# Turning tiles between the slices of the weights product, 32 turns of the identity first, and single loads for the third pair's mixed words

## The chip, the cores and the metric

One Trainium2 chip, one of its NeuronCores. The metric is the device time of one execution of the whole kernel, in microseconds. The core's engines are TensorE (PE), VectorE (DVE), ScalarE (ACT) and GpSimd (POOL); SyncE (SP) issues all DMAs of this kernel, one after the other, and waits on semaphores in between, so that a DMA whose condition isn't met holds all that stand behind it.

## What is computed

Tokens are 2048 rows of 1024 numbers, float32 throughout. The reference, cut to what matters:

```python
xn = _layernorm(x)                                  # over 1024
# gated part
s = silu(xn @ w_gate.T)                             # 2752 columns
# per row, the half of s with the smallest magnitudes is set to 0
idx = top_k(-abs(s), 1376); s[rows, idx] = 0
attn = (s * (xn @ w_up.T)) @ w_down.T
# shared and routed part
logits = xn @ gate_w                                # 8 experts
h = relu(xn @ up_w) ** 2                            # 2048 columns
shared = h @ down_w
routed = ((xn @ fc1_w) @ expert_w * sum(top_k(logits, 2))) @ fc2_w
y = x + attn + (layernorm(shared + routed) * gamma + beta)
```

## The kernel before

Tokens go in four blocks of 512. A block's products run over *granules*: 128 rows of a weight matrix by 512 columns, multiplied by all 512 tokens (four tiles of 128). Full float32 accuracy is had with three passes at the fast float32r rate: each operand is split into a high part (rounded by ScalarE) and a low part (the rest, by GpSimd or VectorE), and `product` (L943 to L947) multiplies high by high, high by low and low by high into one PSUM bank. `plan.granules` is the list of a block's granules in the order of TensorE; the number `m` of a granule in it is what all tables of the program are indexed by. I call it the granule's **place**. Every engine walks over the same places in its own loop and does at each what the tables name there; only semaphores tie the engines together, so VectorE, say, may be some places ahead of TensorE.

**Start.** Before block 0, `expert_w @ fc2_w` (512 x 512 by 512 x 1024) is computed once: the *weights product*. It has two halves of 512 columns (`("weights", 0)` and `("weights", 1)`), each with four slices `k` of 128 inner rows, each slice twelve products over four banks (4 to 7). Slice `k` needs SyncE's loads of `expert_raw` and `fc2_raw` (L620 to L622; the profile calls the latter `fc`), ScalarE's high parts (`first_parts(k)`, L878 to L881) and GpSimd's low parts (L699 to L708). VectorE copies a finished half out of its banks (`first_copy`, L1386). Around it, the first block's four tiles of tokens are normalised by VectorE (`normalise`, L1110, with a square root on ScalarE, `standard`) and turned by TensorE: `turn_token`, eight transposes of 128x128 against the identity `ident`, into banks 0 and 1 or 2 and 3. ScalarE and VectorE then read the turned tile (`first_tokens`, `turn_tokens`). TensorE's order of all this is the list `FIRST` (L187): tiles 0 and 1, the first half, tiles 2 and 3, the second half. `FIRST_AT` counts the banks filled before each entry, for those who wait for them. SyncE loads tile 2 when tile 0 has been turned and tile 3 when tile 1 has (L623 to L625), and all raw weights of block 0 behind that. VectorE's order is: normalise tiles 0 and 1, read turned tiles 0 and 1, normalise 2 and 3, copy the first half, read tiles 2 and 3, copy the second half, then the mixes of block 0.

**Blocks.** Block 0 splits all weights as they come, and stores the split words in `split_w`; blocks 1 to 3 load them from there, one DMA per granule (`load_slot`). In blocks 1 to 3 three pairs of column groups are multiplied by a scheme with seven products of half size in place of eight (Winograd's form of Strassen's): places 8 to 35, 36 to 63 and 64 to 91, seven products of four granules each (`PRODUCTS`), two tiles and six matmuls per granule. Four of the seven take as right operand sums and differences of weight words, T1 to T4, the *mixed* words. For the first two pairs VectorE makes them in block 0 (`mix`). The third pair's are made in block 1: **mixes** 8 to 11, one for each inner granule. For mix `n`, four raw granules are loaded into a quarter of `acc` each (`load_mix`, L577), VectorE combines them in place with four subtractions (`mix_later`, L1163, at the places of `MIX_AT`: 24, 32, 44, 52), and they are stored to `mixed_w` in one DMA (`store_later_mix`, L588). Mixes 8 and 10 share one half of `acc`, 9 and 11 the other, so mix 10's loads wait for mix 8's store, and so on. From place 68 on the mixed words are loaded like others and ScalarE and GpSimd (or VectorE) split them.

SyncE in blocks 1 to 3: it loads the words for the granule whose slot was last used by place `m` when TensorE is through with `m` (in the fast products that is the granule ten places on), and then does `other_loads(b, m)`: what the tables `MIX_LOADS` and `MIX_STORES` name at `m`.

VectorE reads the fast products' banks with `read_fast` six places after a product's last granule. Banks are given by `PRODUCT_BANK`. In the second pair, the third product's banks 6 and 7 (read at place 53, right behind mix 11 at 52) are those that the fifth product opens at place 52.

Of the kernel before, what the change touches and what calls it, by code (L numbers as in the profile page):

```python
# [185 lines left out]

FIRST = [("token", 0), ("token", 1), ("weights", 0), ("token", 2), ("token", 3), ("weights", 1)]  # L187
FIRST_AT, _m = {}, 0
for _key in FIRST:
    FIRST_AT[_key] = _m  # L190
    _m += 2 if _key[0] == "token" else LK
FIRST_FILLS = _m
# [128 lines left out]
MIX_BLOCK = 1  # L321
MIX_LOADS = {8: range(8, 10), 32: range(10, 11), 40: range(11, 12)}
MIX_AT = {24: 8, 32: 9, 44: 10, 52: 11}
MIX_STORES = {26: 8, 34: 9, 46: 10, 54: 11}

# [42 lines left out]
def program(nc, x, w_gate, w_up, w_down, up_w, down_w, fc1_w, expert_w, fc2_w, gamma, beta, routed_w, y):  # L368
    ctx = ExitStack()
    with ctx:  # L370
# [89 lines left out]
        mix_loaded = [sem(f"mix_loaded{i}") for i in range(2)]  # L460
        later_mixes = sem("later_mixes")
        mixes_stored = [sem(f"mixes_stored{i}") for i in range(2)]
        mixed_hi = sem("mixed_hi")
# [95 lines left out]
        def _(sp):  # L559
# [28 lines left out]
            def store_later_mix(n):  # L588
                sp.wait_ge(later_mixes, 4 * (n - FIRST_MIXES) + 4)
                words = acc[:, 2 * (n % 2):2 * (n % 2) + 2, :].rearrange("p t (i n) -> p t i n", n=N)  # L590
                sp.dma_start(mixed_w[n].rearrange("(t i) p n -> p t i n", i=2), words).then_inc(mixes_stored[n % 2], 16)

            def load_slot(g):
                b, m = STREAM[g]
                granule = PLANS[b].granules[m]
                slot_free(sp, g)
                if granule.source[0] == "mixed":
                    _, p, k, i = granule.source
                    n = p * HALF + k
                    sp.wait_ge(mixes_stored[n % 2], 16 * (n // 2 + 1))  # L600
# [34 lines left out]
            def other_loads(b, m):  # L635
                plan = PLANS[b]
                if b == MIX_BLOCK:
                    for n in MIX_LOADS.get(m, ()):
                        load_mix(n)
                    if m in MIX_STORES:  # L640
                        store_later_mix(MIX_STORES[m])
                for t in range(TILES):
# [125 lines left out]
        def _(act):  # L768
# [60 lines left out]
            def read_step(b, name):  # L829
                kind, i = name  # L830
                if kind == "latent":
# [3 lines left out]
                    if b == MIX_BLOCK:  # L835
                        for n in range(2):
                            act.wait_ge(mixes_stored[n], 16 * (MIXES // 2))
                if kind == "routed" and i == 0:
# [103 lines left out]
        def _(pe):  # L942
# [106 lines left out]
            pe.wait_ge(ident_ready, 2)  # L1049
            for kind, i in FIRST:  # L1050
                if kind == "token":
# [4 lines left out]
                    turn_token(i)  # L1056
                else:

                    for k in range(LK):
                        pe.wait_ge(first_lo, 2 * LK + k + 1 if i else 2 * k + 2)  # L1060
                        for t in range(LK):
                            if k == 0 and i:
                                pe.wait_ge(bank_emptied[4 + t], 2)
                            last = product(banks[4 + t][:, :], [p[:, k, t * P:(t + 1) * P] for p in expert],
                                           [p[:, k, i * N:(i + 1) * N] for p in fc2], k == 0, k == LK - 1)
                            if k == LK - 1:
                                last.then_inc(bank_filled, 1)
            for b in range(BLOCKS):
# [25 lines left out]
        def _(dve):  # L1094
# [68 lines left out]
            def mix_later(n):  # L1163

                b11, b21, b12, b22 = (mix_place(n, i) for i in range(4))
                at = 4 * (n - FIRST_MIXES)
                dve.wait_ge(mix_loaded[n % 2], 64 * ((n - FIRST_MIXES) // 2 + 1))
                dve.tensor_tensor(b11, b12, b11, ALU.subtract).then_inc(later_mixes, 1)
# [217 lines left out]
            def first_copy(h):  # L1386

                for t in range(LK):
                    dve.wait_ge(bank_filled, FIRST_AT[("weights", h)] + t + 1)
                    dve.tensor_copy(acc[:, t, h * N:(h + 1) * N], banks[4 + t][:, :]).then_inc(bank_emptied[4 + t], 1)  # L1390
# [114 lines left out]
```

## Time and profile before

| | |
|---|---|
| runs | 2334.61, 2334.75, 2336.58 us; median 2334.75 |
| profiled execution | 2335.83 us, its span 2333.7 us |
| TensorE busy | 2317.7 us (99%) |
| VectorE, ScalarE, GpSimd busy | 1634.8, 1086.9, 829.3 us (70, 47, 36%) |
| DMA | 558.43 MB, mean 239 GB/s; 71.0% of 16 engines' span |
| weights product and first turns | to 38.75 us |
| block 1, places 8 to 91 | 640.7 to about 760 us |

TensorE's records overlap a little (0.39 us long, one every 0.23), so its busy share says when it has work and not how fast it goes; its idle time stands in the waits. The other engines idle a lot, which costs nothing unless TensorE waits for them.

### The profile page before, as it was taken

The page shows a single profiled execution, that of the slowest core. Times are in us where ns is not written, and L with a number is a line of the kernel's source. Part 1 is how long each engine was busy: PE and PEld are TensorE (multiplying, and loading weights), DVE is VectorE, ACT ScalarE, POOL GpSimd, SP SyncE. Part 2 cuts the span into 40 slices and gives each one's busy share as a digit, 9 for nine tenths or more (in the row PEclk, how much of TensorE's full clock was granted, in tenths as well). Part 3 has the DMA queues.
Part 4 walks back from the last instruction along what each step waited for, and adds up shares of the span by engine and source line. Part 5 has one row for each costly group of instructions (what it writes and reads, how often), then busy time and mean ns, then how long its engine had stood idle before and what let it go on. Part 6 is the DMA issues. An engine that isn't in the chain of part 4 may idle for free.

```text
span 2333.7 us, 27748 instructions
## 1 busy us (share of the span) xinstructions
PE 2317.7 (99%) x10504; PEld 1927.2 (83%) x10504; DVE 1634.8 (70%) x1810; ACT 1086.9 (47%) x1253; POOL 829.3 (36%) x682
## 2 busy tenths in 40 slices
PE   8999999999999999999999999999999999999999
PEld 6888888888877888888888888888888888888887
DVE  4349999976265989897334598898723568989850
ACT  3247776223233787722124387761213448785110
POOL 5467878796444021123024321304004413030500
PEclk9999999999999999999999999999999999999999
DMA  7798878878898666665778766665667865556555
GB/s 277 280 394 294 292 245 311 293 243 310 287 363 302 206 196 191 204 201 180 234 237 277 249 194 193 195 209 189 207 219 255 279 221 195 193 192 214 180 190 180
DMA packets 191047, 558.43 MB, mean 239 GB/s; under 512 B 20161, under 2 KB 29377, under 8 KB 190913
## 3 DMA queue, kind: packets, MB, share of 16 engines
q1 hardware_dynamic: 190912, 556.65, 71.0%
q8 instruction: 84, 1.38, 0.2%
q14 instruction: 51, 0.41, 0.1%
HBM read 429.62 MB, written 126.94 MB: 238 GB/s over the span
## 4 chain that ended last, share of the span: by engine, by line
PE 93%; DMA 3%; DVE 1%; SPq 1%; POOL 1%; ACT 0%; issue 0%; DVEq 0%; ACTq 0%
PE bank L945 30%; PE bank L947 30%; PE bank L946 30%; PE bank L965 2%; DMA mixed_w<-mixes 1%; DMA split_w<-w 1%; DMA w<-mixed_w 1%; PE bank L956 1%; POOL w L732 0%; SPq L565 0%; SPq L569 0%; PE bank L1038 0%; PE bank L1039 0%; DMA raw<-w_gate_dram 0%; POOL w L735 0%
## 5 line engine op out<-in xcount | busy, mean ns | idle before, releaser
L1292 DVE TENSOR_SCALAR_CACHE_REDUCE junk_v<-mag,cand 128x2816 bf16<-128x2816 f32 x248 | 780.3, 3146 | 8.8
L786 ACT ACTIVATE junk_s<-mag,cand 128x2816 uint8<-128x2816 f32 x248 | 655.4, 2643 | 222.2 <-DVE cand L1284 195.7
L945 PE MATMUL bank<-w,tok 128*128 128x512 f32 (+1 forms) x952 | 365.8, 384 | 1.8 <-DMA w<-split_w 1.7
L947 PE MATMUL bank<-w,tok 128*128 128x512 f32 (+1 forms) x952 | 364.3, 383 | 0.0
L946 PE MATMUL bank<-w,tok 128*128 128x512 f32 (+1 forms) x952 | 364.1, 382 | 0.0
L732 POOL TENSOR_TENSOR w<-raw,w 128x512 fp32r<-128x512 f32 (+1 forms) x196 | 268.1, 1372 | 77.5 <-ACT w L774 67.8
L945 PE MATMUL bank<-w,prod_t 128*128 128x512 f32 x672 | 269.4, 401 | 0.0
L947 PE MATMUL bank<-w,prod_t 128*128 128x512 f32 x672 | 262.8, 391 | 0.0
L946 PE MATMUL bank<-w,prod_t 128*128 128x512 f32 x672 | 261.9, 390 | 0.0
L945 PE MATMUL bank<-tok,w 128*128 128x512 f32 x640 | 249.0, 389 | 0.0
L946 PE MATMUL bank<-tok,w 128*128 128x512 f32 x640 | 249.0, 389 | 0.0
L947 PE MATMUL bank<-tok,w 128*128 128x512 f32 x640 | 249.0, 389 | 0.0
L744 POOL TENSOR_TENSOR squares<-squares 128x512 f32<-128x512 f32 x64 | 67.2, 1050 | 494.4 <-ACT hidden L874 494.3
L759 POOL TENSOR_TENSOR prod<-prod,mag 128x512 f32<-128x512 f32 x88 | 126.5, 1460 | 285.9 <-DVE prod L1357 285.6
L934 ACT ACTIVATE prod_t<-bank 128x512 fp32r<-128x512 f32 x88 | 52.4, 596 | 337.0 <-PE bank L965 337.0
L945 PEld LDWEIGHTS bank<-w,tok 128*128 128x128 f32 x952 | 178.7, 188 | 34.2 <-DMA w<-split_w 2.1
L947 PEld LDWEIGHTS bank<-w,tok 128*128 128x128 f32 x952 | 178.7, 188 | 32.5
L946 PEld LDWEIGHTS bank<-w,tok 128*128 128x128 f32 x952 | 178.8, 188 | 31.5
L945 PE MATMUL bank<-w,hidden 128*128 128x512 f32 x512 | 199.3, 389 | 0.0
L946 PE MATMUL bank<-w,hidden 128*128 128x512 f32 x512 | 199.2, 389 | 0.0
L947 PE MATMUL bank<-w,hidden 128*128 128x512 f32 x512 | 199.2, 389 | 0.0
L735 POOL TENSOR_TENSOR w<-w 128x512 fp32r<-128x512 f32 x78 | 117.0, 1524 | 143.8 <-ACT w L906 143.6
(149 smaller groups left out, 3728.3 us busy)
## 6 DMA issues: line engine op xcount, KB each, us to landing
w<-split_w SPq DMA_DIRECT2D x516, 512.0 KB, 3.5
split_w<-w SPq DMA_DIRECT2D x192, 512.0 KB, 4.9
w_more<-split_w SPq DMA_DIRECT2D x60, 512.0 KB, 5.2
w<-mixed_w SPq DMA_DIRECT2D x108, 256.0 KB, 3.5
rows<-x_dram SPq DMA_DIRECT2D x32, 512.0 KB, 4.9
raw<-w_down_dram SPq DMA_DIRECT2D x44, 256.0 KB, 3.9
raw<-w_up_dram SPq DMA_DIRECT2D x40, 256.0 KB, 3.1
w<-split_w SPq DMA_DIRECT2D x24, 392.0 KB, 3.5
```

The costliest lines, as they stand in the source:

```text
L732: pool.tensor_tensor(lo, words, hi, ALU.subtract).then_inc(lo_ready, 1)
L735: pool.tensor_tensor(slot_of(g)[:, 1, :], slot_of(g)[:, 1, :].bitcast(F32), slot_of(g)[:, 0, :], ALU.subtract).then_inc(pool_lo, 1)
L744: pool.tensor_tensor(squares[:, n, :], squares[:, n, :], squares[:, n, :], ALU.mult).then_inc(squared, 1)
L759: pool.tensor_tensor(prod[:, c, :, units], prod[:, c, :, units], mag[:, c, :, units], ALU.mult).then_inc(prod_ready, 1)
L786: act.activation(junk_s[:, :, :], mag[:, :, t, :], ACT.Sign, scale=-1.0, bias=cand[:, t:t + 1], accum_out=cnt[:, t:t + 1]).then_inc(counte ...
L934: act.activation(prod_t[0][:, c, :], banks[bank][:, :], ACT.Copy).then_inc(operand_hi, 1)
L945: pe.matmul(out, left[0], right[0], start=first, stop=False)
L946: pe.matmul(out, left[0], right[1], start=False, stop=False)
L947: return pe.matmul(out, left[1], right[0], start=False, stop=last)
L956: last = pe.transpose(banks[2 * (t % 2) + h][:, k * P:(k + 1) * P], rows_of(t)[:, (h * HK // 2 + k) * P:(h * HK // 2 + k + 1) * P], ident[ ...
L965: last = pe.transpose(banks[bank][:, t * P:(t + 1) * P], prod[:, c, t, :], ident[:, :])
L1292: dve.tensor_scalar(junk_v[:, :, :], mag[:, :, t, :], cand[:, t:t + 1], float(1 - (GATED - KEPT)), ALU.is_lt, ALU.add, accum_out=cnt[:, t: ...
```

## The change

Three things, with the numbers of the tables:

1. `FIRST` names the slices of the weights product one by one: tile 0, slice 0, tile 1, slices 1 to 3, tile 2, slice 0 of the second half, tile 3, its slices 1 to 3. ScalarE splits slice 0 before the second tile's square root, and slice 2 before it reads the first turned tile.
2. Ahead of all of it TensorE turns the identity 32 times into bank 3 (`WARM`); nobody reads the result.
3. The loads of a mix's four granules are single entries of `MIX_LOADS` at places of their own, and so are the four stores, each with its own DMA. The later mixes have semaphores of their own (`later_stored`), 64 counts per mix.

```diff
-FIRST = [("token", 0), ("token", 1), ("weights", 0), ("token", 2), ("token", 3), ("weights", 1)]
+WARM = 32
+FIRST = [("token", 0), ("weights", 0, 0), ("token", 1), ("weights", 0, 1), ("weights", 0, 2), ("weights", 0, 3),
+         ("token", 2), ("weights", 1, 0), ("token", 3), ("weights", 1, 1), ("weights", 1, 2), ("weights", 1, 3)]
...
-    _m += 2 if _key[0] == "token" else LK
+    _m += 2 if _key[0] == "token" else LK if _key[2] == LK - 1 else 0
...
-MIX_LOADS = {8: range(8, 10), 32: range(10, 11), 40: range(11, 12)}
+MIX_LOADS = {4: (8, 0), 5: (8, 1), 6: (8, 2), 7: (8, 3), 10: (9, 0), 13: (9, 1), 16: (9, 2), 19: (9, 3),
+             31: (10, 0), 33: (10, 1), 35: (10, 2), 37: (10, 3), 39: (11, 0), 41: (11, 1), 43: (11, 2), 45: (11, 3)}
 MIX_AT = {24: 8, 32: 9, 44: 10, 52: 11}
-MIX_STORES = {26: 8, 34: 9, 46: 10, 54: 11}
+MIX_STORES = {at + 2 * i: (n, i) for n, at in ((8, 21), (9, 29), (10, 44), (11, 52)) for i in range(4)}
...
-            def load_mix(n):
+            def load_mix(n, i):
...
-                    sp.wait_ge(mixes_stored[n % 2], 16 * (n // 2))
-                for i in range(4):
-                    src, width = words_of((PAIRS[p][i // 2], k + i % 2 * HALF))
-                    sp.dma_start(mix_place(n, i), src).then_inc(mix_loaded[n % 2], 16)
-
-            def store_later_mix(n):
+                    sp.wait_ge(later_stored[n % 2], 64 * later_round(n))
+                src, width = words_of((PAIRS[p][i // 2], k + i % 2 * HALF))
+                sp.dma_start(mix_place(n, i), src).then_inc(mix_loaded[n % 2], 16)
+
+            def store_later_mix(n, i):
                 sp.wait_ge(later_mixes, 4 * (n - FIRST_MIXES) + 4)
-                words = acc[:, 2 * (n % 2):2 * (n % 2) + 2, :].rearrange("p t (i n) -> p t i n", n=N)
-                sp.dma_start(mixed_w[n].rearrange("(t i) p n -> p t i n", i=2), words).then_inc(mixes_stored[n % 2], 16)
+                sp.dma_start(mixed_w[n, i], mix_place(n, i)).then_inc(later_stored[n % 2], 16)
...
             standard(0, 0)
+            first_parts(0)
             standard(1, 1)
-            first_parts(0)
             first_parts(1)
+            first_parts(2)
             first_tokens(0)
-            first_parts(2)
             first_parts(3)
             first_tokens(1)
...
             pe.wait_ge(ident_ready, 2)
-            for kind, i in FIRST:
+            for n in range(WARM):
+                pe.transpose(banks[3][:, 0:P], ident[:, :], ident[:, :])
+            for kind, i, *slices in FIRST:
...
-                else:
-
-                    for k in range(LK):
-                        pe.wait_ge(first_lo, 2 * LK + k + 1 if i else 2 * k + 2)
-                        for t in range(LK):
-                            if k == 0 and i:
-                                pe.wait_ge(bank_emptied[4 + t], 2)
+                for k in slices:
+                    pe.wait_ge(first_lo, 2 * LK + k + 1 if i else 2 * k + 2)
+                    for t in range(LK):
+                        if k == 0 and i:
+                            pe.wait_ge(bank_emptied[4 + t], 2)
```

ScalarE's first instructions before, where `expert_62` and `fc_0_64` are the high parts of a slice's two operands and `tok` reads a turned tile:

```order
L779 ACTIVATE std<-var 128x1 x2
L880 ACTIVATE expert_62<-expert_raw 128x512
L881 ACTIVATE fc_0_64<-fc_raw 128x1024
L880 ACTIVATE expert_62<-expert_raw 128x512
L881 ACTIVATE fc_0_64<-fc_raw 128x1024
L800 ACTIVATE tok<-bank 128x4x128 x2
L880 ACTIVATE expert_62<-expert_raw 128x512
L881 ACTIVATE fc_0_64<-fc_raw 128x1024
```

and in the changed kernel:

```order
L792 ACTIVATE std<-var 128x1
L893 ACTIVATE expert_62<-expert_raw 128x512
L894 ACTIVATE fc_0_64<-fc_raw 128x1024
L792 ACTIVATE std<-var 128x1
L893 ACTIVATE expert_62<-expert_raw 128x512
L894 ACTIVATE fc_0_64<-fc_raw 128x1024
L893 ACTIVATE expert_62<-expert_raw 128x512
L894 ACTIVATE fc_0_64<-fc_raw 128x1024
L813 ACTIVATE tok<-bank 128x4x128 x2
```

Slice 0 has moved past a square root, and slice 2 past the reads of the first turned tile; the fourth slice and the reads of the second tile follow in both.

SyncE's queue in block 1 from the last plain words before the fast products on, before (`acc` are the mixes' loads):

```order
L604 DMA w<-split_w 128x1024 x4
L601 DMA w<-mixed_w 128x512 x2
L601 DMA w_more<-mixed_w 128x512 x2
L604 DMA w_more<-split_w 128x1024 x2
L604 DMA w<-split_w 128x1024
L586 DMA acc<-w_gate_dram 128x512 x2
L586 DMA acc<-w_up_dram 128x512 x2
L586 DMA acc<-w_gate_dram 128x512 x2
L586 DMA acc<-w_up_dram 128x512 x2
L604 DMA w<-split_w 128x1024
```

and in the changed kernel:

```order
L597 DMA acc<-w_gate_dram 128x512
L617 DMA w<-split_w 128x1024
L597 DMA acc<-w_gate_dram 128x512
L614 DMA w<-mixed_w 128x512
L597 DMA acc<-w_up_dram 128x512
L614 DMA w<-mixed_w 128x512
L597 DMA acc<-w_up_dram 128x512
L614 DMA w_more<-mixed_w 128x512 x2
L617 DMA w_more<-split_w 128x1024 x2
L617 DMA w<-split_w 128x1024 x2
L614 DMA w<-mixed_w 128x512
L597 DMA acc<-w_gate_dram 128x512
```

The eight loads in a row stood between the words of places 18 and 19; now mix 8's stand between those of places 10 to 14, and mix 9's come later, one by one.

The same queue around places 43 to 46, in the changed kernel (`mixed_w<-acc` are a mix's stores):

```order
L597 DMA acc<-w_up_dram 128x512
L617 DMA w_more<-split_w 128x1024
L601 DMA mixed_w<-acc 128x512
L617 DMA w_more<-split_w 128x1024
L597 DMA acc<-w_up_dram 128x512
L614 DMA w_more<-mixed_w 128x512
L601 DMA mixed_w<-acc 128x512
```

The first store of mix 10 (place 44) now stands ahead of the last load of mix 11 (place 45); before, all of mix 11's loads stood ahead of mix 10's store.

## Rows read from the trace of the kernel before

**Rows 1.** The page: chain of work that ended last, share of the span by engine.

```profile
PE 93%; DMA 3%; DVE 1%; SPq 1%; POOL 1%; ACT 0%; issue 0%; DVEq 0%; ACTq 0%
```

**Rows 2.** Waits of TensorE, whole run: engine, what, releaser: us in total, times, longest.

```profile
PE bank L956 <- DVE rows L1115: 8.8, 2, 7.8
PE bank L945 <- DMA w<-split_w: 1.7, 1, 1.7
PE bank L945 <- POOL w L735: 1.6, 2, 1.0
```

**Rows 3.** Busy time of TensorE by stretch: length, busy (count), clock, DMA share, GB/s.

```profile
13.00:17.28 4.28, 4.21 (x10) 1.00 1.03 368
28.00:38.70 10.70, 10.70 (x48) 1.00 0.26 98
```

**Rows 4.** Timeline of TensorE, start: start us, us, engine, line, what, count, [idle before].

```profile
10.71 1.97 PE L956 MATMUL bank<-ident,rows 128*128 128x128 f32 x8 [0.93 <-DVE rows L1115]
13.07 0.80 PE L945 MATMUL bank<-fc,expert 128*128 128x512 f32 x1 [0.39 <-POOL fc L707]
...
38.75 0.39 PE L945 MATMUL bank<-w,tok 128*128 128x512 f32 x1
```

**Rows 5.** Timeline of ScalarE, start.

```profile
9.52 0.61 ACT L880 ACTIVATE expert<-expert_raw 128x512 fp32r<-128x512 f32 x1
...
16.34 1.08 ACT L800 ACTIVATE tok<-bank 128x512 fp32r<-128x512 f32 x2
```

**Rows 6.** DMA issues of SyncE between 2.0 and 2.5 us: KB, us to landing.

```profile
fc_raw<-fc_w_dram SPq DMA_DIRECT2D x1, 512.0 KB, 6.3
```

**Rows 7.** Timeline of GpSimd, start.

```profile
10.21 1.57 POOL L703 TENSOR_TENSOR expert<-expert_raw,expert 128x512 fp32r<-128x512 f32 x1 [8.74 <-ACT expert L880]
11.75 1.26 POOL L707 TENSOR_TENSOR fc<-fc_raw,fc 128x512 fp32r<-128x512 f32 x1
```

**Rows 8.** Timeline of VectorE, start.

```profile
18.16 1.28 DVE L1099 BATCH_NORM_STATS2 stats<-rows 128x6 f32<-128x512 f32 x2
...
25.17 2.47 DVE L1390 COPY acc<-bank 128x512 f32<-128x512 f32 x4
```

**Rows 9.** Timeline of SyncE's queue, block 1: first load of the burst, load after it.

```profile
643.65 0.68 SPq L586 DMA_DIRECT2D acc<-w_gate_dram  x1
...
648.50 0.44 SPq L604 DMA_DIRECT2D w<-split_w  x1
```

**Rows 10.** DMA issues of SyncE between 648.45 and 648.55 us.

```profile
w<-split_w SPq DMA_DIRECT2D x1, 512.0 KB, 9.2
```

**Rows 11.** Timeline of TensorE, block 1: places 19, 20, 38, 46 and 52.

```profile
657.75 0.50 PE L945 MATMUL bank<-w,tok 128*128 128x512 f32 x1 [1.69 <-DMA w<-split_w]
...
660.44 0.50 PE L945 MATMUL bank<-w,sums 128*128 128x512 f32 x1 [1.03 <-POOL w L735]
...
685.05 0.39 PE L945 MATMUL bank<-w,tok 128*128 128x512 f32 x1
...
695.93 0.39 PE L945 MATMUL bank<-w_more,tok 128*128 128x512 f32 x1
...
704.79 0.47 PE L945 MATMUL bank<-w,sums 128*128 128x512 f32 x1 [0.31 <-DVE mag L1192]
```

**Rows 12.** DMA issues of SyncE at 678.8, 682.5 and 691.5 us, in this order.

```profile
acc<-w_gate_dram SPq DMA_DIRECT2D x1, 256.0 KB, 5.2
...
w_more<-split_w SPq DMA_DIRECT2D x1, 512.0 KB, 9.8
...
acc<-w_gate_dram SPq DMA_DIRECT2D x1, 256.0 KB, 5.8
```

**Rows 13.** Timeline of VectorE, block 1: first and last of mix 10, first of mix 11.

```profile
686.66 0.69 DVE L1168 TENSOR_TENSOR acc<-acc 128x512 f32<-128x512 f32 x1 [1.26 <-DMA acc<-w_up_dram]
...
690.79 0.69 DVE L1173 TENSOR_TENSOR acc<-acc 128x512 f32<-128x512 f32 x1
...
699.97 1.04 DVE L1168 TENSOR_TENSOR acc<-acc 128x512 f32<-128x512 f32 x1 [4.89 <-DMA acc<-w_up_dram]
```

More of the change, by code:

```diff
@@ L321, with later_round @@
 MIX_BLOCK = 1
-MIX_LOADS = {8: range(8, 10), 32: range(10, 11), 40: range(11, 12)}
+MIX_LOADS = {4: (8, 0), 5: (8, 1), 6: (8, 2), 7: (8, 3), 10: (9, 0), 13: (9, 1), 16: (9, 2), 19: (9, 3),
+             31: (10, 0), 33: (10, 1), 35: (10, 2), 37: (10, 3), 39: (11, 0), 41: (11, 1), 43: (11, 2), 45: (11, 3)}
 MIX_AT = {24: 8, 32: 9, 44: 10, 52: 11}
-MIX_STORES = {26: 8, 34: 9, 46: 10, 54: 11}
+MIX_STORES = {at + 2 * i: (n, i) for n, at in ((8, 21), (9, 29), (10, 44), (11, 52)) for i in range(4)}
+def later_round(n):
+    return (n - FIRST_MIXES) // 2
 MIX_PLACE = [0, 3, 2, 1]
@@ L461, in program @@
         later_mixes = sem("later_mixes")
+        later_stored = [sem(f"later_stored{i}") for i in range(2)]
         mixes_stored = [sem(f"mixes_stored{i}") for i in range(2)]
@@ L599, in load_slot @@
                     n = p * HALF + k
-                    sp.wait_ge(mixes_stored[n % 2], 16 * (n // 2 + 1))
+                    if n < FIRST_MIXES:
+                        sp.wait_ge(mixes_stored[n % 2], 16 * (n // 2 + 1))
+                    else:
+                        sp.wait_ge(later_stored[n % 2], 64 * (later_round(n) + 1))
                     sp.dma_start(slot_of(g)[:, 1, :].bitcast(F32), mixed_w[n, MIX_PLACE[i]]).then_inc(slot_loaded[SLOT[g]], 16)
@@ L637, in other_loads @@
                 if b == MIX_BLOCK:
-                    for n in MIX_LOADS.get(m, ()):
-                        load_mix(n)
+                    if m in MIX_LOADS:
+                        load_mix(*MIX_LOADS[m])
                     if m in MIX_STORES:
-                        store_later_mix(MIX_STORES[m])
+                        store_later_mix(*MIX_STORES[m])
                 for t in range(TILES):
@@ L836, in read_step @@
                         for n in range(2):
-                            act.wait_ge(mixes_stored[n], 16 * (MIXES // 2))
+                            act.wait_ge(later_stored[n], 64 * ((MIXES - FIRST_MIXES) // 2))
                 if kind == "routed" and i == 0:
@@ L1056, in _ @@
                     turn_token(i)
-                else:
-                    for k in range(LK):
-                        pe.wait_ge(first_lo, 2 * LK + k + 1 if i else 2 * k + 2)
-                        for t in range(LK):
-                            if k == 0 and i:
-                                pe.wait_ge(bank_emptied[4 + t], 2)
[L1064 to L1067, printed above, removed]
+                for k in slices:
[3 more added lines that the diff above has]
+                            pe.wait_ge(bank_emptied[4 + t], 2)
+                        last = product(banks[4 + t][:, :], [p[:, k, t * P:(t + 1) * P] for p in expert],
+                                       [p[:, k, i * N:(i + 1) * N] for p in fc2], k == 0, k == LK - 1)
+                        if k == LK - 1:
+                            last.then_inc(bank_filled, 1)
             for b in range(BLOCKS):
@@ L1166, in mix_later @@
                 at = 4 * (n - FIRST_MIXES)
-                dve.wait_ge(mix_loaded[n % 2], 64 * ((n - FIRST_MIXES) // 2 + 1))
+                dve.wait_ge(mix_loaded[n % 2], 64 * (later_round(n) + 1))
                 dve.tensor_tensor(b11, b12, b11, ALU.subtract).then_inc(later_mixes, 1)
@@ L1388, in first_copy @@
                 for t in range(LK):
-                    dve.wait_ge(bank_filled, FIRST_AT[("weights", h)] + t + 1)
+                    dve.wait_ge(bank_filled, FIRST_AT[("weights", h, LK - 1)] + t + 1)
                     dve.tensor_copy(acc[:, t, h * N:(h + 1) * N], banks[4 + t][:, :]).then_inc(bank_emptied[4 + t], 1)
```

## The prediction, made before the result was known

> **What bounds the kernel now.** Read first the chain of work that ended last: TensorE holds 93% of it [rows 1], so only time in which TensorE stands still or runs slowly can be won. The list of TensorE's waits for the whole run shows how little that is: 1.7 us for a DMA of words, 1.6 us for GpSimd's low parts in two waits [rows 2], and 0.3 us for a bank [rows 11]. The span is TensorE's own work but for the start and these few places, and the change touches just these: the start, and block 1, where all of them but 8.8 us at the very start [rows 2] lie. A gain can be a few microseconds of 2334.75. A measurement of this kernel can tell about 0.2% (4.7 us) from no change.
>
> At the start, TensorE turns two tiles, waits for the first slice of the weights product until 13.07, and block 0 begins at 38.75 [rows 4]. The stretches say at which clock: ten products fit between 13.00 and 17.28, 0.43 us apart, which is the level of 1.2 GHz for 512 columns, and 48 later ones take 10.70 us, 0.22 apart, the level of 2.4 GHz [rows 3]. The clock column reads 1.00 in both, so here the steps must be believed and not the column. Sixteen turns ran before 13.07, eight from 7.8 on, after TensorE's longest wait, and eight from 10.71 to 12.68 [rows 2, 4]; at 1.97 us for eight they filled 3.9 of 4.9 us, and the products behind them were still slow.
>
> **The start, costed.** ScalarE now splits slice 0 before the second tile's square root. It used to begin at 9.52 [rows 5]; the slice's second load, issued at 2.12, lands 6.3 us later, at 8.4 [rows 6]. So the split begins at 8.45, 1.1 earlier. GpSimd follows: its two subtractions per slice take 1.6 and 1.3 us, and it waited for ScalarE at 10.21 [rows 7]; slice 0 is complete near 11.8 in place of 13.0. Each later slice costs it 2 x 1.26 = 2.5 us, less than TensorE's 12 x 0.227 = 2.7 (the spacing of [rows 11]), so TensorE runs: slice 0 to 14.5, turn of tile 1 (8 turns, half of the slow 1.97 of [rows 4]: 1.0) to 15.5, slices 1 to 3 to 23.6, turn of tile 2 to 24.6. This holds if the clock is at 2.4 GHz from 11.8 on, which is what the 32 turns of the identity can give; they fill 32 x 0.25 = 7.9 us at the slow level (1.97 for 8 [rows 4]), from about 1.5 to at most 9.4, and delay nothing, since slice 0 is what the products wait for.
>
> Then something else is late: the first slice of the second half needs banks that VectorE empties in its copy at 25.17 [rows 8]. VectorE comes to it through ScalarE's copy of the second turned tile at 16.34 [rows 5], which stands behind all four splits and the last load, before and after, and then through the two normalisations that began at 18.16 [rows 8]. That path doesn't move. So TensorE stands from 24.6 to about 25.8 (0.6 for the first copied bank), and then has one slice, one turn, three slices: 2.7 + 1.0 + 8.0 = 11.7, to 37.6 in place of 38.75. **Start: -1.1 us.** ScalarE begins the splits of block 0's words some 2 us later, as tile 3 is turned behind a slice; the first is needed at 37.6 and they take 8 us from 30, so this is hidden; it would cost its 2 us only if they ended at the bound. The load of tile 3 waits for the turn of tile 1 and goes out near 15.5; its user begins near 22, so also hidden.
>
> **The weights mix, costed.** In block 1 the words of the third pair are combined while the fast products run; eight granules there last 10.88 us, 685.05 to 695.93 [rows 11], 0.227 for each of their 48 products. I call a granule's number in the block's stream its place, as the tables of the diff do. Before, the eight loads of mixes 8 and 9 go out in one burst, 643.65 to 648.50, ahead of a load of words that goes out only then [rows 9] and takes 9.2 us to land [rows 10]. TensorE meets it: it stands 1.69 at 657.75 and 1.03 at 660.44 [rows 11], and as products start 0.227 apart while a record lasts 0.39, each wait is 0.16 longer than its row: 3.0 us together. With single loads at places 4 to 7 and 10 to 19 the same load goes out 5 us earlier. **-3.0 us at this place.** The stores are now 16 in place of 4: 12 more issues by 0.44 [rows 9] are 5 us of SyncE's queue over 70 us, beside its waits for free slots. The bytes are the same.
>
> **What is late next** is the mixing itself. The last loads of mixes 10 and 11 used to be issued at places 32 and 40, now at 37 and 45, and VectorE does mix 10 before its read at place 49 and mix 11 before its read at place 53, which empties the bank that TensorE opens at place 52. With TensorE 3.0 earlier, follow it. Place 38 began at 685.05 [rows 11], now 682.05; SyncE issues the last load of mix 10 at 682.5. The queue then holds everything that it held before: landings were 5.2 us at 678.8, and 9.8 at 682.5 behind a store [rows 12]. I take 7.0, between them and nearer to the first, since the stores are quarters now. It lands at 689.5. Mixing took from 686.66 to 691.48, 4.8 [rows 13]: to 694.3. Here is the new wait: SyncE's store at place 44 is due from 691.5 and is held for that mixing until 694.3, and behind it on the same queue stands the load at place 45. It goes out at 695.2 (a store and a load of words before it), lands in 5.8 as a load after such a pause did [rows 12], at 701.0, and from the start of mix 11 to the place that waits for the bank were 4.8 us (699.97 to 704.79) [rows 11, 13]. Place 52 then begins at 705.8, against 704.79. So the 3.0 us are not kept: at place 52 TensorE is 1.0 **behind**. Without SyncE's pause it would be place 46's start, 695.93 - 3.0 = 692.9, + 0.4 + 5.8 + 4.8 = 703.9, so even then only 0.9 is kept.
>
> Further on, the second wait for GpSimd (0.6 in the row of [rows 2], the total less 1.03, and 0.16) came at the end of a run of reads on VectorE that began late for words; these land earlier relative to TensorE after such a stand, and it goes: -0.75. **Block 1: +0.25.**
>
> The sum is -1.1 + 1.0 - 0.75 = -0.85 against the profiled execution's own 2335.83 us, hence 2335.0. That execution lies 1.1 over the median of the three runs, 2334.75, so the forecast on that scale is 2333.9. Blocks 2 and 3 are unchanged. In block 0 the mixes start with VectorE's copy of the last slice, so they move with TensorE and keep the 1.1.
>
> **Bounds of what isn't shown.** For block 1 below: landing 5.2, mixing four operations of 0.69 [rows 13] plus 0.8 for the read, gives place 52 near 702.2, a gain of 2.6. Above: landing 9.8 puts the rest 2.8 later, +3.8, and the wait for GpSimd may then stay.
>
> **Rivals.** (A) *The queue is shorter* than I take it, since no burst fills it: place 52 at 702.2 to 703.9, and the gain of the first place stays in part. For it: single loads meet 5.2 to 5.8 [rows 12]. Against: the landing of 9.2 [rows 10] and 9.8 shows that the queue was full through this region, and the bytes are the same. Block 1 then gives 1.6 to 3.4 and the total is -2.7 to -4.5: about 2331.2. Chance 0.27.
> (B) *SyncE's pause decides, slower than before.* The load at place 45 is held by the store at 44, that by mixing, that by the load at 37, and this by a full queue. Where: place 52. It turns the change into a loss from a landing over 7.9 (the forecast's 7.0 and its 0.85) for the last load of mix 10. At 9.8 it costs +3.8 and with the start's -1.1 the total is +2.7 to +3.5: about 2337.8. For it: the 9.8 at just that time. Chance 0.17.
> (C) *The turns of the identity don't raise the clock*, so that part of the change doesn't do what it is there to do. For it: sixteen turns before 13.07, and slow products behind. Against: they had pauses between them, and 32 don't. Then slice 0 is slow: ten products by 0.43 and two fast ones end it at 16.5, the turn of tile 1 at 17.5, ScalarE's copy comes 0.6 late and with it VectorE's path; block 0 starts at 38.2. If the clock rises no sooner than before, 17.28, it is 39.1. The start gives -0.5 to +0.3, not -1.1, and the total on the forecast's branch is near 2334.9. Chance 0.45, beside A and B and the forecast, which is independent of it. The Trainium skill, TensorE: Matmul & The Clock Gate, section on PE-mode transpose, says that a transpose doesn't count as busy for the full clock as a product does; by that rule C is what happens. The slow products behind the sixteen turns agree with it but don't settle it.
>
> **How the numbers follow.** The forecast, both gains at the ends small and the chain of mixing taking back the middle, has 0.56, A 0.27, B 0.17. The range takes the lower bound (-4.5) less the start's doubt, and B without its worst: 2330.7 to 2337.9. Faster by over 0.2% needs A at its bound with the clock up: 0.12. Slower by over 0.2% needs B at its bound with C: 0.05. Within 0.2%: 0.83.
>
> **What would show it.** Right: products 0.227 apart from slice 0 on; TensorE idle by about 1.2 before the second half's first slice, released by VectorE's copy; block 0 at 37.6; no wait at places 19 and 20; one new wait of 3 to 5 us near 700 to 706 for VectorE's read of the bank; SyncE's store of mix 10 held behind its mixing. Wrong: products 0.43 apart from 11.8 (C); place 52 with a wait under 2.5 us (A), or over 6 (B); a wait at another place of the fast products would break the argument as a whole.

## The result and the profile after

| | before | after |
|---|---|---|
| median, 22 runs each on one chip | 2336.01 us | 2339.71 us |
| lowest, highest | 2334.61, 2338.29 | 2337.28, 2342.59 |
| ratio, 95% interval | | 1.0016 [1.001, 1.0022] |
| profiled execution, its span | 2335.83, 2333.7 us | 2342.59, 2340.5 us |

The change costs 3.7 us. Forecast was a gain of 0.85; the upper end of the range, 2337.9, lies 3.15 over the 2334.75 that it was counted from, so the loss is outside it by either count. The interval is that of the ratio of the two kernels' times. The profiled execution of after is its slowest run, 2.9 over its median, so its trace shows more loss than a usual run has.

The page of after, chain of work that ended last, answers to [rows 1] and hardly differs:

```profile
PE 93%; DMA 3%; SPq 1%; DVE 1%; ACT 1%; POOL 1%; issue 0%; DVEq 0%; ACTq 0%
```

TensorE's waits over the whole run (us in total, times, longest) answer to [rows 2]:

```profile
PE bank L958 <- DVE mag L1205: 4.2, 1, 4.2
...
PE bank L958 <- POOL w L745: 2.8, 3, 1.3
...
PE bank L958 <- POOL w_more L748: 1.6, 1, 1.6
PE bank L958 <- POOL w L748: 0.6, 1, 0.6
```

The DMA wait of 1.7 is gone; in its place stands one of 4.2 on VectorE's reading of a bank, and behind the start there are five on GpSimd's low parts, 5.0 us together. The timeline of TensorE says where they are:

```profile
2.02 6.01 PE L1064 MATMUL bank<-ident 128*128 128x128 f32 x32 [2.02 <-POOL ident L709]
...
11.74 0.50 PE L958 MATMUL bank<-fc,expert 128*128 128x512 f32 x1 [2.84 <-POOL fc L720]
...
25.16 0.47 PE L958 MATMUL bank<-fc,expert 128*128 128x512 f32 x1 [0.44 <-DVE acc L1403]
...
141.07 0.44 PE L958 MATMUL bank<-w,tok 128*128 128x392 f32 x1 [1.26 <-POOL w L745]
...
653.89 0.50 PE L958 MATMUL bank<-w_more,sums 128*128 128x512 f32 x1 [1.59 <-POOL w_more L748]
...
704.74 0.77 PE L958 MATMUL bank<-w,sums 128*128 128x512 f32 x1 [4.21 <-DVE mag L1205]
```

I laid the starts of the same places beside those of before. Each row says what after has more or less there; "so" gives how far it is behind by then:

| where | change, us |
|---|---|
| block 0 begins at 37.07 (38.75) | -1.7 |
| block 0, to place 8 of block 1 at 643.01 (640.72) | +4.0, so +2.3 |
| places 13 and 14, GpSimd, late words | +2.75 |
| places 19 to 21, the waits of [rows 11] gone | -3.3, so +1.7 |
| **place 48**, waits for VectorE's read | +4.4 |
| places 48 to 50, TensorE at 1.2 GHz | +2.5, so +8.6 |
| places 51 to 60, the wait at 52 gone | -1.0 |
| places 71 to 73, GpSimd's second wait gone | -1.0 |
| end at 2336.95 (2330.11) | +6.8 |

Place 48 is the largest piece. VectorE's timeline there:

```profile
695.97 0.69 DVE L1181 TENSOR_TENSOR acc<-acc 128x512 f32<-128x512 f32 x1 [7.80 <-DMA acc<-w_up_dram]
...
697.89 1.67 DVE L1186 TENSOR_TENSOR acc<-acc 128x512 f32<-128x512 f32 x1
699.49 2.31 DVE L1222 TENSOR_SCALAR positive<-mag 128x2048 uint8<-128x2048 f32 x1
701.83 2.17 DVE L1226 TENSOR_SCALAR mag<-mag 128x2048 int32<-128x2048 int32 x1
703.92 1.28 DVE L1205 TENSOR_TENSOR mag<-bank,mag 128x512 f32<-128x512 f32 x2
```

Mix 10 waits for its last load; behind mix 10 stand two instructions on the signs of `mag` (2.31 and 2.17), and only then the read at place 49 of VectorE's loop, which empties the banks that TensorE opens at place 48. SyncE's queue and that load's landing:

```profile
687.33 0.48 SPq L597 DMA_DIRECT2D acc<-w_up_dram  x1
...
699.59 0.32 SPq L601 DMA_DIRECT2D mixed_w<-acc  x1
...
700.43 0.47 SPq L597 DMA_DIRECT2D acc<-w_up_dram  x1
```

```profile
acc<-w_up_dram SPq DMA_DIRECT2D x1, 256.0 KB, 8.6
```

The load goes out at 687.33 and lands 8.6 later. The store at place 44 is held until 699.59, when mix 10 is done, and mix 11's last load stands behind it: the pause that rival B describes is there, but TensorE had met an earlier bank. Stretches of TensorE (length, busy, clock, DMA share, GB/s):

```profile
11.74:14.50 2.76, 2.76 (x12) 1.00 0.98 396
...
698.00:704.60 6.60, 2.54 (x12) 0.89 1.03 408
704.60:709.90 5.30, 5.16 (x12) 0.50 0.70 232
709.90:716.00 6.10, 6.10 (x28) 1.00 0.72 219
```

After the wait, twelve products start in 5.3 us: 1.2 GHz, from 703.1 to 709.9 by the clock's record. The first row is slice 0 of the weights product: twelve in 2.76 us, 2.4 GHz, right behind the 32 turns, the first tile's turn and a pause of 2.84.

### The profile page after: what moved, and what is told of

It is laid out like the page before. It is cut to its first block, busy times and chain, and to the rows that moved or that the text cites. A ratio compares the mean times of both kernels' runs of the same rounds, so it can differ in the third digit from the quotient of the medians.

```text
span 2340.5 us, 27823 instructions
## 1 busy us (share of the span) xinstructions
PE 2322.4 (99%) x10536; PEld 1932.2 (83%) x10536; DVE 1635.9 (70%) x1810; ACT 1086.3 (46%) x1253; POOL 829.7 (35%) x682
## 4 chain that ended last, share of the span: by engine, by line
PE 93%; DMA 3%; SPq 1%; DVE 1%; ACT 1%; POOL 1%; issue 0%; DVEq 0%; ACTq 0%
PE bank L958 30%; PE bank L960 30%; PE bank L959 30%; PE bank L978 2%; DMA split_w<-w 1%; DMA mixed_w<-mixes 1%; PE bank L969 0%; SPq L577 0%; POOL w L745 0%; DMA acc<-w_up_dram 0%; DMA fc_raw<-fc_w_dram 0%; PE bank L1052 0%; PE bank L1051 0%; DMA raw<-w_gate_dram 0%; SPq L581 0%
## 6 DMA issues: line engine op xcount, KB each, us to landing
w<-split_w SPq DMA_DIRECT2D x516, 512.0 KB, 4.2
split_w<-w SPq DMA_DIRECT2D x192, 512.0 KB, 5.0
w_more<-split_w SPq DMA_DIRECT2D x60, 512.0 KB, 5.5
rows<-x_dram SPq DMA_DIRECT2D x32, 512.0 KB, 5.4
```

## Experiments

Two theories were on the table. **T1:** the later loads of mix 10 (last at place 37 in place of 32) make the loss, by mixing, signs and read, and the clock adds to it. **T2:** it comes from the start, whose gain is lost in block 0 for another reason.

Kernels were measured in jobs, each on one chip with the kernel before beside them; "against" names that job's median of before, and differences between two jobs are taken over it.

**The parts alone.** e1_start has `FIRST`, the ScalarE order and the 32 turns; e2_mix only the tables and semaphores of the mixes; e3_no_turns is e1 with

```diff
-WARM = 32
+WARM = 0
```

> Only the start of the change (slices between turned tiles, 32 turns of the identity, ScalarE's order), the mixes as before. In the changed kernel's trace block 0 began 1.7 us earlier (37.07 against 38.75) but block 1's place 8 came 2.3 us later (643.01 against 640.72), with waits at 111, 121, 127 and 141 us. Theory 1: block 0 is held by its chain of stores, mixes and loads, which doesn't follow TensorE, and the 4.0 us lost there are the start's doing: block 0 begins at 37.1, waits of 3 us or more before 145 us, time 1 to 3 us above the kernel before. Rival: the loss in block 0 is chance of that one execution (landings differ from run to run): the gain is kept in part and the time is 0 to 1.7 us below the kernel before.

> Only the change of the mixes (single loads and stores), the start as before. Theory 1: the waits at places 19 and 20 go (-3.2 us), place 48 waits 3 to 5 us for VectorE's read behind mix 10, and such a wait lets TensorE's clock fall to 1.2 GHz for some 7 us, 3 us more: in all 0 to +4 us against the kernel before, depending on whether an execution's clock falls. Rival: most of the changed kernel's loss is the start's in block 0, and the mixes alone are equal to the kernel before or up to 2 us faster.

> As e1 but without the 32 turns of the identity. If the turns raise the clock: products of slice 0 are 0.43 apart without them and 0.23 with them, and block 0 begins 0.5 to 2 us later than in e1. If they don't, both are alike. Whatever block 0 begins at, theory 1 (block 0 held by its own chain) expects the time to differ from e1 by less than 1 us; the rival expects the whole difference of the start in the time.

Against 2335.31: e1 2337.10, ratio 1.0009 [1.0000, 1.0018]; e2 2336.16, 1.0005 [0.9996, 1.0014]; e3 2335.88, 1.0003 [0.9994, 1.0012]. No part alone makes the 3.7; their costs, 1.8 and 0.85, add up to 2.6, and the last 1.1 between the jobs is not explained. Without the turns, e3 is 1.2 below e1, more than the "less than 1 us" of theory 1, and the waits in e1's block 0 are 1.9 us and not 3 or more. TensorE's timeline of e2:

```profile
648.23 0.50 PE L954 MATMUL bank<-w_more,sums 128*128 128x512 f32 x1 [0.62 <-POOL w_more L744]
...
698.42 0.77 PE L954 MATMUL bank<-w,sums 128*128 128x512 f32 x1 [3.55 <-DVE mag L1201]
```

and its stretch behind that wait:

```profile
697.60:704.40 6.80, 5.98 (x14) 0.50 0.84 292
```

So the wait at place 48, the half clock for 6.8 us and most of the small wait near place 13 (0.24 in e3) belong to the mix part; the block 0 losses (waits of 0.44 and 1.46 near 125 and 139) to e1. In e3 these two are absent, though slices and ScalarE's order are in.

**The mixing's loads sooner.** e4_sooner is e2 with

```diff
-             31: (10, 0), 33: (10, 1), 35: (10, 2), 37: (10, 3), 39: (11, 0), 41: (11, 1), 43: (11, 2), 45: (11, 3)}
+             31: (10, 0), 32: (10, 1), 33: (10, 2), 34: (10, 3), 39: (11, 0), 40: (11, 1), 41: (11, 2), 42: (11, 3)}
```

and e7_all_sooner is the whole change with it. e5_filled is e2 with ten idle products ahead of place 48:

```diff
+                if b == 1 and m == 48:
+                    bank, value = emptied(b, ("fast", 0, 6, 0))
+                    pe.wait_ge(bank_emptied[bank], value)
+                    for n in range(FILL):
+                        pe.matmul(banks[bank][:, :], tok[0][:, 0, 0:P], tok[0][:, 0, :], start=True, stop=True)
```

e6_turns is before with the 32 turns and nothing else.

> As e2, with the loads of mix 10 at places 31 to 34 and of mix 11 at 39 to 42, in place of every second place up to 37 and 45. Theory 1: the last load of mix 10 lands some 4 us sooner, VectorE reads the bank before place 48 opens it, no wait there over 1 us and no fall of the clock; time 2 to 4 us below the kernel before and below e2. Rival: the queue is so full that the loads land no sooner, or the wait moves to place 52: time as e2.

> As e2, with ten products of a token slice by itself at place 48, into a bank that is free there and whose content nobody reads; TensorE does them while it would stand still for VectorE's read (3.6 us in e2's trace), ten by 0.23 = 2.3 us. Nothing is read sooner by it. Theory 1 (the wait lets the clock fall, and the fall is half of the loss): the idle time left is 1.3 us, no stretch at 1.2 GHz in the trace, time 2 to 3.5 us below e2. Rival (the fall has another cause, or costs nothing): the clock falls again near 700 us and the time is e2's.

> The kernel before with nothing but the 32 turns of the identity ahead. They raise the clock (in e1's trace it rose at 6.8 us), so slice 0's products are 0.23 apart and block 0 begins near 36.7 to 37.4 in place of 38.75. Theory 3: the chain of mixes in block 0 (first mixed store to eighth: 78.7 to 79.2 us in the four traces without turns, 80.6 and 81.5 in the two with them) takes longer where TensorE is ahead of it, so nothing is gained: time 0 to +2.5 us. Rival: what costs time in e1 are the slices and ScalarE's order, and the turns alone gain 1 to 2 us.

> The changed kernel as it is, with e4's places for the loads of mixes 10 and 11 (31 to 34 and 39 to 42). Theory 1 (costs add up): no wait over 1.5 us at place 48, no fall of the clock, and the time is e4's plus what e1 costs over the kernel before: -3.7 + 1.8, so 1 to 3 us below the kernel before, and 4 to 6 below the changed kernel. Rival: with TensorE early at the start the mixes are late again and the time is over the kernel before's.

e4: 2331.64 against 2335.31, ratio 0.9984 [0.9975, 0.9993], **3.7 us faster than before** and 4.5 than e2. e7, the whole change with the same places: 2332.92 against 2335.41, 0.9990 [0.9981, 0.9999], 2.5 below before where the change as it was is 3.7 above. Six loads issued one to three places sooner turn the loss into a gain. VectorE in e4:

```profile
686.48 0.69 DVE L1177 TENSOR_TENSOR acc<-acc 128x512 f32<-128x512 f32 x1 [3.97 <-DMA acc<-w_up_dram]
...
689.02 1.22 DVE L1218 TENSOR_SCALAR positive<-mag 128x2048 uint8<-128x2048 f32 x1
690.28 1.23 DVE L1222 TENSOR_SCALAR mag<-mag 128x2048 int32<-128x2048 int32 x1
691.42 1.28 DVE L1201 TENSOR_TENSOR mag<-bank,mag 128x512 f32<-128x512 f32 x2
```

and TensorE's waits in it, but for the start:

```profile
PE bank L954 <- POOL w_more L744: 1.1, 2, 0.8
PE bank L954 <- DVE mag L1201: 0.9, 1, 0.9
```

The read at place 49 is at 691.42 (703.92 in the changed kernel, 697.60 in e2); no wait at 48, no fall of the clock. T1 holds for the larger part of the loss. The loads alone don't make the whole distance. In e2 and in the changed kernel VectorE's last mixing instruction takes 1.67 and the two on signs 4.4, while GpSimd makes four subtractions in a row beside them; in e4 GpSimd idles from 686.3 to 694.0, and they take 0.69 and 2.4. So about 3 us of VectorE's lateness is time beside GpSimd, and only the rest is the load's landing (8.0 in e2, 6.9 in e4) and issue.

GpSimd in the changed kernel:

```profile
697.35 7.77 POOL L748 TENSOR_TENSOR w<-w 128x512 fp32r<-128x512 f32 x4 [5.38 <-ACT w L919]
```

e5: 2335.41 against 2335.41, 1.0004 [0.9995, 1.0013]. The products keep the clock at 2.4 GHz, yet the bound at place 52 shows behind it:

```profile
697.21 2.43 PE L1004 MATMUL bank<-tok 128*128 128x512 f32 x10
699.81 0.50 PE L955 MATMUL bank<-w,sums 128*128 128x512 f32 x1 [0.17 <-DVE mag L1207]
...
707.19 0.47 PE L955 MATMUL bank<-w,sums 128*128 128x512 f32 x1 [1.67 <-DVE mag L1207]
```

So what the clock costs can't be had back alone: in e2 it covers the wait at place 52. From place 48 to 53, e5 takes 8.8 us and e2 9.7: of the 2.5 us of the slow stretch 0.9 comes back. By medians, e5 is 0.85 us nearer to its before than e2 is to its own, in two jobs and within their intervals; I had expected 2 to 3.5. The clock's own price in the median stays open.

e6: 2338.31 against 2335.41, 1.0014 [1.0005, 1.0023]: **the turns alone cost about 3 us**, a little over the 0 to 2.5 of theory 3, and far from the gain of its rival. They do raise the clock; its stretches in e6:

```profile
5.60:12.40 6.80, 4.02 (x33) 1.00 1.02 399
12.40:15.80 3.40, 2.94 (x7) 0.50 1.02 407
15.80:19.20 3.40, 3.40 (x16) 1.00 1.05 389
```

**Better loads, and what the turns do.** e8_spread is e4 with mixes 8 and 9 at other places; e9_sooner_slices is e7 without turns; e10_tiny has 32 products of two columns of the identity in place of the turns of e6; e11_turns_again is e6.

```diff
-MIX_LOADS = {4: (8, 0), 5: (8, 1), 6: (8, 2), 7: (8, 3), 10: (9, 0), 13: (9, 1), 16: (9, 2), 19: (9, 3),
+MIX_LOADS = {10: (8, 0), 12: (8, 1), 14: (8, 2), 16: (8, 3), 18: (9, 0), 20: (9, 1), 22: (9, 2), 24: (9, 3),
```

> The mix part alone with the sooner loads of mixes 10 and 11, and mixes 8 and 9 loaded at places 10, 12, 14, 16 and 18, 20, 22, 24 in place of 4 to 7 and 10, 13, 16, 19. If the wait of 0.6 to 1.6 us that every kernel of the mix part shows near place 13 comes from the four loads of mix 8 at places 4 to 7, which stand ahead of the words of places 8 to 14, it goes, no wait comes at places 19 to 21, and the median is 0.8 to 1.5 us below that of the sooner loads: 2330.1 to 2331.0, that is 4.3 to 5.2 below the kernel before. If it comes from the words alone (the queue full with the loads of ten places ahead), the wait stays and the median is that of the sooner loads, 3.7 below before.

> The whole change with the sooner loads, but without the 32 turns of the identity. If the turns are what costs in the start part, this is the sooner loads' time and no more: 3.2 to 3.7 us below before, 1 us below the same kernel with turns (2.5 below before in its job). If the slices cost by themselves, it is as slow as with turns, 2.5 below before or less.

> The kernel before with 32 products of the identity by two of its columns at the start, in place of 32 whole turns: the same number of instructions of TensorE ahead of everything, but 2 columns in place of 128 each. If the turns cost by their instructions (code is loaded at other moments of block 0), this is as slow as the turns alone, 2 to 3 us above before, with waits of 1.3 us near 139. If they cost by the clock that they raise and the earlier start of block 0, this is the kernel before: within 1 us, clock rising near 17, block 0 starting near 38.5.

> The kernel before with the 32 turns alone, once more, to see whether the 2.9 us that it lost in its first job (2338.31 against 2335.41) stands. If turns cost: 1.5 to 3 us above before again. If that was scatter between jobs: within 1 us of before.

All against 2335.05. e8: 2332.60, 0.9987 [0.9978, 0.9996]: the wait near place 13 went, as expected, but two others came, on VectorE's low parts (1.49 at 674.15, 0.70 at 677.86), so nothing was won over e4: 2.4 below before, where 4.3 to 5.2 was expected. e9: 2331.83, 0.9984 [0.9975, 0.9993], 3.2 below before to e4's 3.7: what the slices cost or give is lost in the scatter. e11: 2338.37, 1.0010 [1.0001, 1.0019]: the turns cost again, 3.3 by medians and 2.3 by the ratio. With the slices in, they cost less: 1.2 (e1 against e3), 0.7 (e7 against e9). e10: 2342.76, 1.0031 [1.0020, 1.0042], but it tells little: its 32 products stand in the trace as 64 matmuls, so they aren't as many instructions as the turns; they ran for 13.8 us, to 15.80, and pushed the first tile's turn to 15.66 from 7.84; block 0 began 4.1 late for that alone.

The profiled execution of e11 begins block 0 at 40.71, that of the same kernel in e6 at 37.90. VectorE's third normalisation in e11, then in e6:

```profile
20.20 5.64 DVE L1117 TENSOR_SCALAR rows<-rows,mv,rstd 128x1024 f32<-128x1024 f32 x1
```

```profile
20.19 1.89 DVE L1117 TENSOR_SCALAR rows<-rows,mv,rstd 128x1024 f32<-128x1024 f32 x1
```

while GpSimd in e11 ran five subtractions without a break:

```profile
19.00 6.28 POOL L707 TENSOR_TENSOR fc<-fc_raw,fc 128x512 fp32r<-128x512 f32 x5
```

**GpSimd kept away from it.** In e12 (to e6), e13 (to before), e14 (to e4) and e15 (to e7):

```diff
+                    if h == 1 and k == 0:
+                        pool.wait_ge(tokens_ready, 3)
```

> The kernel before with the 32 turns, and GpSimd waits for VectorE's third normalisation before its first subtraction of the second half. If the 3 us of the turns are VectorE's normalisation held beside GpSimd (5.64 us in one profile), they go: that instruction takes 0.8 to 1.0, block 0 begins at or before 37.0, no run is above 2338, and the median is within 1 us of before, 2335. If the turns cost by what comes later in block 0, the median stays 2 to 3 us above before.

> The kernel before with that wait of GpSimd alone. The third normalisation takes 0.8 in place of 1.9 us and the fourth tile is turned 1 us sooner, which TensorE doesn't wait for: the median is that of before within 0.8 us. If the slow runs of before (2338 to 2340, 4 of 29 in the last job) are such a hold, none is above 2337.5 here.

> The sooner loads of the mix part (3.7 below before) with the same wait of GpSimd. As for the kernel before: same median within 0.8 us, 3.2 to 4.5 below before, and no run far above the others if the hold makes these.

> The whole change with sooner loads (2.5 below before in its job) and the same wait of GpSimd. If the hold is what the turns cost, this is the fastest kernel of all, since it keeps what the start gives: 4 to 5 below before. If the turns cost in block 0, it stays at 2 to 3 below before.

Against 2335.16: e12 2337.87, 1.0010 [1.0001, 1.0019]; e13 2334.93, 0.9999 [0.9990, 1.0008]; e14 **2331.13**, 0.9982 [0.9973, 0.9991]; e15 2333.18, 0.9989 [0.9980, 0.9998]. The third normalisation takes 0.81 to 0.82 in all four profiles, and the turns still cost 2.7 (e12); the turns, slices and ScalarE's order together cost 2.0 (e15 against e14). The hold is real but isn't what they cost. e14 has the lowest median of all, its highest run 2332.34.

**Work or mere instructions?** e16_waits has, in place of the turns, 64 waits that are met already; e17_turns_waits has the turns and these waits.

```diff
-            for n in range(32):
-                pe.transpose(banks[3][:, 0:P], ident[:, :], ident[:, :])
+            for n in range(64):
+                pe.wait_ge(ident_ready, 2)
```

> The kernel before with 64 waits that are met already in TensorE's program, where the turns stood: as many instructions, no work, no clock. If the turns cost by their instructions, this has the wait of 1.2 to 1.6 us for GpSimd near 140, the interval from the fifth to the sixth mixed store of block 0 is 13.3 or more (12.2 to 12.6 without turns), and the median is 2 to 3 us above before. If they cost by the clock or by the start's order, it is the kernel before: no such wait, interval 12.2 to 12.6, median within 1 us.

> The 32 turns and the 64 met waits behind them. If the instructions' places in the program matter, the moments at which code is loaded shift again and the wait near 140 changes with them, in size or in place; if the clock or the early start matters, it stays at 1.2 to 1.6 us near 140 and the median at 2 to 3 us above before, as in the two jobs of the turns alone.

Against 2335.31: e16 2336.09, 1.0004 [0.9994, 1.0013]; e17 2336.23, 1.0001 [0.9992, 1.0010]. TensorE in e16, then in e17:

```profile
143.52 0.50 PE L945 MATMUL bank<-w,tok 128*128 128x512 f32 x1 [1.09 <-POOL w L732]
```

```profile
138.37 0.44 PE L945 MATMUL bank<-w,tok 128*128 128x392 f32 x1 [1.37 <-POOL w L732]
```

Sixty-four instructions without any work bring a wait for GpSimd near 140, as every profile with the turns has it (1.2 to 1.6), and e10 (0.79 at 143.65); before, e2, e3, e4, e8, e13 and e14 have none, e5 and e9 one of 0.15 and 0.21. And 64 such waits *behind* the turns bring the loss from 2.9 and 3.3 us down to 0.9, though the turns still raise the clock and that wait near 140 is still there. This speaks against the raised clock and the turns' work as the whole price. It isn't a price by the instruction either: e16 costs 0.8, within its interval, where 2 to 3 was expected, its interval from the fifth to the sixth store is 12.85 and not 13.3, and e17, with more instructions ahead than either, costs 0.9. So what stands at the head of TensorE's program seems to matter by where it puts the rest. The ratios' intervals of e17 and of e6 and e11 overlap, so this is supported and not settled.

The traces have one thing that moves so. The profile's DMA queue 8 brings instructions, 16 KB at a time, one every 23 to 32 us in the first 170. Its second load begins at 56.0 to 57.7 us in the nine traces with nothing ahead of the first turn, at 51.8 in e16, at 46.8 to 50.5 in the seven with turns, at 48.5 in e10, and at 42.0 in e17. That shows loads of code coming sooner; it doesn't show that one of them delays anything, and by what link the turns cost stays open.

## Why the prediction was wrong

**The start.** Right in its steps, and near in size: clock up, slice 0 at 11.74 (11.8), products 0.23 apart, block 0 at 37.07 (37.6). TensorE's idle time before the second half was 0.44, not 1.2, since VectorE's copy came at 24.33 in place of 25.17. Rival C is refuted in every profile with turns: the record rises at 5.5 to 7.6 us in place of 14.7 to 17.5 (19.5 in e10). The rule that I weighed there, of the Trainium skill, TensorE: Matmul & The Clock Gate, section on PE-mode transpose, doesn't hold for these float32 turns. They don't keep what they gain in every case: in e6, e11, e12 and e15 the clock fell again at 12.3 to 12.6 for 3.4 us, while TensorE waited for slice 0 or, in e15, 0.6 us after that wait had ended. The size of the gain is in part luck: 38.75, from which it was counted, is the latest start of block 0 in the eight profiles that keep the start's order of before and have no turns (37.57 is the earliest).

**"They move with TensorE and keep the 1.1": failed.** Block 0 does not follow TensorE's start. Before, SyncE's fifth and sixth of the eight stores of mixed words, and the last:

```profile
103.00 0.46 SPq L574 DMA_DIRECT2D mixed_w<-mixes  x1
...
115.17 0.49 SPq L574 DMA_DIRECT2D mixed_w<-mixes  x1
...
129.73 0.65 SPq L574 DMA_DIRECT2D mixed_w<-mixes  x1
```

and after:

```profile
102.83 0.48 SPq L586 DMA_DIRECT2D mixed_w<-mixes  x1
...
116.99 0.50 SPq L586 DMA_DIRECT2D mixed_w<-mixes  x1
...
131.55 0.67 SPq L586 DMA_DIRECT2D mixed_w<-mixes  x1
```

Place 8 of block 1 follows the last of these by 510.3 to 512.0 us in all nineteen traces, wherever block 0 began. So the time is lost ahead of it. The first of the eight was 0.7 earlier than before, the last 1.8 later. The interval from the fifth store to the sixth is 12.0 to 12.9 in the eleven traces without turns, and 13.3 to 14.2 in six of the eight with them (not in e6, 12.50, and e17, 11.89). The chain of work between the fifth and the sixth store differs. Before, it runs through the landing of the fifth mixed store, whose place VectorE's next mixing takes; its row:

```profile
103.00 7.02 DMA mixed_w<-mixes
```

After, it runs through the landing of a store of split words, then ScalarE, GpSimd and SyncE's queue, and so it does in e1, e7, e12 and e15, but not in e6, e11 and e17:

```profile
105.85 7.93 DMA split_w<-w
```

Why that store is on the chain with turns in most traces no run shows. I costed the turns at nothing because they delay nothing at the start; the price came 100 us later, and what carries it is open.

**"Place 52": failed.** I followed mix 11 to its reader and didn't follow mix 10 to its own. The landing that I took as 7.0 was 8.6, inside my bounds; what decides is the omission. By the prediction's own clock mixing ends at 694.3; two sign instructions stand behind it in VectorE's loop, which no term of mine held (4.5 us here, 2.5 in e4), then 0.8 for the read. The bank is free at 697.6 to 699.6, while TensorE reaches place 48 at 695.6, two granules behind my 692.9 for place 46. That is a wait of 2.0 to 4.0 at place 48, and 4.21 was measured. The rows of VectorE that I quoted stop just ahead of these instructions. The forecast had set its own test, that a wait at another place than 52 would break the argument, and this is that wait.

**The clock: missing.** I priced a wait at its own length. With a wait of 4.21 (3.55 in e2) the clock fell to 1.2 GHz for 6.8 us; in the changed kernel products ran in the last 5.2 of these. That cost 2.5 us more.

**Right:** the 3.0 at places 19 and 20 (3.3) and the second wait for GpSimd (1.0 for 0.75) went; the store of mix 10 held behind its mixing. New and not foreseen: 2.75 at places 13 and 14, where mix 8's loads now stand ahead of words that are due; e8, with them later, lacks that wait. So of the 3.3 won at places 19 and 20 only 0.55 was left by place 21, before anything of place 48. Rival B's total, 2337.8, lies nearest to what came (3.1 over its 2334.75, to 3.7 measured), but by luck: the pause of SyncE that it rests on was there, and TensorE had lost its time at place 48 before it reached place 52. Its sum isn't sound at the top either: 3.8 less 1.1 is +2.7 with the second wait for GpSimd kept, and no term of it makes +3.5.

## What to carry to other kernels

When a load is moved later, follow its consumer through everything that stands behind it on the same engine, to the first buffer that another engine opens, and do so for each load, not only for the last. Look also at what another engine does beside that chain: here GpSimd's work beside VectorE made up a good part of the delay. A gain at the start of a phase is one at its end only if the phase's slowest chain starts with it. Treat a gain of a few microseconds as unproven until it has been measured against a kernel that differs only in dead instructions.

## What the hardware showed

- Transposes of a 128x128 float32 identity raise TensorE's clock: 32 of them in 5.4 to 6.4 us, the record rising 3.5 to 5.6 us after the first.
- Waits of 3.55 (e2) and 4.21 us (after) inside block 1 came with 6.8 us at 1.2 GHz, one of 3.61 us (e10) with 3.4 us, and ones of 1.7 us (before, e5) with none. The length of the wait alone doesn't decide: at the start, 2.85 us ahead of slice 0 was followed by a fall in e15, 2.84 us in the changed kernel was not. In profiles with the start of before the first rise lay anywhere from 14.7 to 17.3 us, and block 0 began at 37.57 (rise at 14.7), 38.02 (15.9), 38.25 (16.3), 38.62 (17.1) and 38.75 (17.3): part of the scatter between runs.
- VectorE's third normalisation, 128x1024 float32 from and to SBUF, took 0.81 where GpSimd waited for it, 1.1 to 1.9 beside GpSimd's subtractions, and once 5.64, until five of them were through. The fourth took 0.81 in before, beside the same subtractions, so not every instruction there is held. The sign instructions took 1.22 with GpSimd idle (e4) and up to 2.31 beside it (e2, after).
- 64 instructions without work at the head of TensorE's program came with a wait of 1.09 some 130 us later (e16) and, behind the turns, with a median about 2 us lower (e17).
